# Output projection of a gated recurrent layer in half-precision parts, with a cast on ScalarE and a subtraction on GpSimd

## The chip, the core and the metric

The kernel runs on one core of a Trainium2 chip. Its time is the device time of one launch in microseconds (us), the median over several runs. The engines are TensorE (PE, and PEld for its weight loads), VectorE (DVE), ScalarE (ACT), GpSimd (POOL) and SyncE (SP). Each works through its own instruction stream in order, and the streams meet only at semaphores: an instruction may wait until a semaphore has reached a number, and may raise one when it is done.

## The reference, cut to what matters

The input x has 32 sequences of 128 positions with 256 features. A recurrent attention stand-in runs over the positions, then a mixture-of-experts feed-forward part follows.

```python
def step(carry, xs):                       # once for each of 128 positions
    r, state = carry
    r = decay * r + kt * vt
    retained = (qt * r).reshape(B, D)
    inp = retained @ Wi.T + bi
    gate = sigmoid(inp @ Wg.T + bg)
    blended = gate * state + (1.0 - gate) * inp
    state = tanh(blended @ A.T + inp @ Bm.T)
    out = state @ Wo.T + bo                # the projection that is changed
    return (r, state), out

x = x + tanh(g_xattn) * recurrence(layernorm(x), ctx, ctx)
x = x + tanh(g_ffn) * ffn(layernorm(x))
# ffn: silu(a) * b of a shared layer, times w_shared_out, plus the two best
# of eight experts on silu(a) * b of w1
```

## The kernel before, in words

**Tiles and iterations.** A tile is 8 positions of all 32 sequences: 256 tokens. There are 16. Data lie features on partitions, as two chunks of 128 features by 256 tokens, 128x512 in all. Iteration i works on several tiles at once: the eight recurrent steps of tile i; the input, gate and Bm products of tile a = i + 1, which don't depend on the state; the Wo projection, the second layer norm and the first shared product of tile c = i - 1; the rest of the feed-forward part of tile d = i - 2; and the first layer norm of tile f = i + 2. The last three tiles compute all experts (`DENSE`), the others scatter their rows to DRAM by expert, multiply block by block (`duo`, L621) and gather the results.

**The order.** The order on each engine is written out by hand in that engine's function `iteration`. Between two recurrent steps TensorE has filler work. After step 0 come the first half of w1 (L850) and perhaps a duo, after step 1 the Wo product (L862 to L869) and w1's second half (L872), which waits for `hs_ready`, after step 7 the second half of sh and the gate logits (L965 to L980).

**A recurrent step.** ScalarE makes the new state with a tanh (`tanh_step`, L999). VectorE makes from it u_hi (half precision), u_full and u_lo (`gated_state`, L1312). TensorE adds eight products with u_hi and four with u_lo to the addends in PSUM (`recurrence`, L593, lines 602 and 607).

**Half-precision parts.** Most products take their operands as hi + lo, two half-precision parts each, and sum hi x hi, hi x lo and lo x hi: `token_product` (L582, for tokens on the output's partitions) and `feature_product` (L567). The parts of an activation are made by a cast on ScalarE (hi) and a subtraction (lo), which is done on GpSimd by its helper `low` (L1856, the subtraction is line 1857) or on VectorE. The Wo product is an exception: float32 state times `whole_wo`, the float32 weights turned and scaled by ScalarE in the setup (L1169).

**Around the change.** ScalarE, behind the eighth tanh, takes the silu of the shared product into `sil_s` (L1274), in iterations 2 and 3 also a scale and a cast of w2 (`w2_high`, L1108). At the next iteration's start it presets the bank of the Wo product with the bias (`wo_preset`, L1031). VectorE, behind `gated_state(i, 7)`, does the routing sums (`rows`, in four iterations), the scan of the decaying memory (`scanned`, L1440, line 1445) and, in some iterations, additions of gathered rows (`combine_second`); in the next iteration it makes `hs` (L1671) behind `gated_state(i, 1)` and x1 from the Wo product (`projected`, L1482) behind `gated_state(i, 2)`. GpSimd starts the scatters (L1914) and gathers (L1927) at set steps (`moves`, L1952), each behind that step's tanh, and between them makes hs_lo (L1970), the low parts of hid (L1982, L1984) and, in iterations 2 to 4, those of w2 (`w2_low`, L1868).

## Time and profile before

| | |
|---|---|
| median of 3 runs | 471.37 us (470.33 to 474.23) |
| profiled execution | 472.12 us, its span 470.4 us |
| TensorE busy | 419.8 us, 89% |
| VectorE busy | 363.8 us, 77% |
| ScalarE busy | 226.1 us, 48% |
| GpSimd busy | 192.4 us, 41% |
| granted TensorE clock, mean | 0.985 of full speed |
| DMA | 63.08 MB, mean 134 GB/s |

A busy share is an average over the whole span. It says how much an engine does, not whether the end waits for it. What a shorter or a longer instruction is worth is read from the timeline around it: what the next instruction of each engine waited for. In a timeline row the first number is the start in us from the span's start, the second the duration in us; a bracket at the end gives the engine's idle time before the row and what ended it. Matmuls overlap each other, so their starts tell the pace and not their durations.

### The profile page before, as it was taken

The numbers are of one execution on the slowest core, as the hardware profiler recorded it, in microseconds if no ns is written. First come the engines' busy times: TensorE is split into PE (matmuls) and PEld (weight loads), VectorE is DVE, ScalarE is ACT, GpSimd is POOL, SyncE is SP. The second block draws the span as 40 slices with busy tenths as digits, with TensorE's granted clock in tenths as the row PEclk, the third lists the DMA queues.
The fourth block names the chain that finished last, engine by engine and source line by source line (L and its number), as shares of the span: only waits on it lengthen the run. The fifth ranks groups of instructions, "written<-read, shape, count | busy, mean of one in ns | idle before, by whom it ended". The sixth has DMA issues, their size and how long they took to land.

```text
span 470.4 us, 12307 instructions
## 1 busy us (share of the span) xinstructions
PE 419.8 (89%) x4348; PEld 353.8 (75%) x4348; DVE 363.8 (77%) x1305; ACT 226.1 (48%) x526; POOL 192.4 (41%) x231
## 2 busy tenths in 40 slices
PE   5987699999989999999999989997997998989891
PEld 4875487787878888889788878896986875766650
DVE  2687989999998887667988877769786569558784
ACT  3564556676655463546455546354653233321400
POOL 3011312432437530202275664431577463707551
PEclk9999899999999999999999999999999899999997
DMA  7795023325051655843423179793234859698862
GB/s 171 198 247 158 2 47 113 93 65 147 24 152 64 180 102 106 151 118 102 102 70 101 47 164 175 192 181 114 102 113 107 186 154 196 167 220 227 199 207 100
DMA packets 110283, 63.08 MB, mean 134 GB/s; under 512 B 80400, under 2 KB 100240, under 8 KB 110224
## 3 DMA queue, kind: packets, MB, share of 16 engines
q1 hardware_dynamic: 105104, 48.66, 43.6%
q0 software_dynamic: 5120, 13.64, 10.2%
q8 instruction: 36, 0.59, 0.5%
q14 instruction: 23, 0.19, 0.1%
HBM read 24.26 MB, written 27.53 MB: 110 GB/s over the span
## 4 chain that ended last, share of the span: by engine, by line
PE 46%; DVE 26%; issue 7%; DMA 6%; ACT 3%; POOL 3%; POOLq 0%; DVEq 0%; ACTq 0%
PE bank L577 9%; PE bank L588 9%; PE bank L635 9%; PE rec L719 4%; DVE u_hi L1324 4%; PE rec L602 4%; DVE u_full L1326 3%; DMA raw_sh<-hrows 2%; DVE r L1445 2%; PE rec L577 2%; PE bank L867 2%; PE rec L607 2%; DMA raw_w<-hrows 2%; PE bank L680 2%; DVE hs L1671 1%
## 5 line engine op out<-in xcount | busy, mean ns | idle before, releaser
L1004 ACT ACTIVATE state<-rec 128x64 f32<-128x64 f32 x128 | 36.7, 287 | 116.9 <-PE rec L607 115.7
L1914 POOL DMA_INDIRECT hrows<-hid_rows,slots_i x52 | 56.8, 1093 | 70.1 <-ACT state L1004 30.1
L1324 DVE SCALAR_TENSOR_TENSOR u_hi<-gt,state 128x64 f16<-128x64 f32 x127 | 43.0, 339 | 44.0 <-ACT state L1004 43.5
L1927 POOL DMA_INDIRECT yg<-yrows,slots_i x52 | 53.5, 1029 | 49.9 <-DMA yrows<-squares_sh 18.6
L602 PE MATMUL rec<-u_hi,a_hi 128*128 128x32 f16 x512 | 47.8, 195 | 14.7 <-DVE u_hi L1324 14.7
L602 PEld LDWEIGHTS rec<-u_hi,a_hi 128*128 128x128 f16 x512 | 37.0, 98 | 21.5 <-DVE u_hi L1324 19.0
L602 PE MATMUL rec<-u_hi,a_lo 128*128 128x32 f16 x512 | 47.5, 194 | 0.0
L1857 POOL TENSOR_TENSOR hs_lo<-hs,hs_hi 128x512 f16<-128x512 f32 x14 | 16.2, 1158 | 54.0 <-ACT hs_hi L1214 53.9
L607 PE MATMUL rec<-u_lo,a_hi 128*128 128x32 f16 x512 | 36.5, 194 | 1.6 <-DVE u_lo L1329 0.7
L1326 DVE SCALAR_TENSOR_TENSOR u_full<-gt,state 128x64 f32<-128x64 f32 x127 | 36.9, 290 | 0.0
L602 PEld LDWEIGHTS rec<-u_hi,a_lo 128*128 128x128 f16 x512 | 35.2, 98 | 1.6 <-issue 0.6
L577 PE MATMUL bank<-xn_hi,sh_hi 128*128 128x256 f16 x128 | 34.9, 273 | 0.0
L577 PE MATMUL bank<-xn_lo,sh_hi 128*128 128x256 f16 x128 | 34.9, 273 | 0.0
L577 PE MATMUL bank<-xn_hi,sh_lo 128*128 128x256 f16 x128 | 34.9, 273 | 0.0
L867 PE MATMUL bank<-whole_wo,state 128*128 128x256 f32 x128 | 32.9, 402 | 0.0
L1864 POOL TENSOR_TENSOR rs<-ve,minus_half 128x2 f32<-128x2 f32 x16 | 12.3, 770 | 49.5 <-DVE nm L1513 49.5
L635 PE MATMUL bank<-w_hi,raw_w 128*128 x144 | 27.2, 276 | 5.5 <-issue 3.3
L1329 DVE TENSOR_TENSOR u_lo<-u_full,u_hi 128x64 f16<-128x64 f32 x127 | 28.7, 226 | 4.3
L588 PE MATMUL bank<-w_hi,xn_hi 128*128 128x256 f16 x104 | 28.5, 274 | 3.0 <-DVE hs L1671 2.9
L719 PE MATMUL rec<-cn,whole_a 128*128 128x256 f32 x128 | 31.2, 387 | 0.0
L588 PE MATMUL bank<-w_lo,xn_hi 128*128 128x256 f16 x104 | 28.4, 273 | 0.0
L588 PE MATMUL bank<-w_hi,xn_lo 128*128 128x256 f16 x104 | 28.4, 273 | 0.0
(299 smaller groups left out, 1383.2 us busy)
## 6 DMA issues: line engine op xcount, KB each, us to landing
yrows<-squares_w SPq DMA_DIRECT2D x20, 256.0 KB, 3.0
yrows<-squares_sh SPq DMA_DIRECT2D x18, 256.0 KB, 3.1
x_sb<-in_x_dram SPq DMA_DIRECT2D x16, 256.0 KB, 3.4
c_sb<-in_ctx_dram SPq DMA_DIRECT2D x64, 64.0 KB, 3.1
xr_sb<-in_x_dram SPq DMA_DIRECT2D x16, 256.0 KB
hrows<-zeros SPq DMA_DIRECT2D x4, 1024.0 KB, 5.9
raw_w<-in_L_ffn_w_dram SPq DMA_DIRECT2D x8, 256.0 KB, 4.8
out_dram<-raw_w SPq DMA_DIRECT2D x8, 256.0 KB, 2.5
```

The lines of the kernel that those rows point to most:

```text
L577: last = pe.matmul(o, w[:, kc, at], a[:, kc, :], start=first, stop=(kc == KC - 1 and w is w_lo), skip_group_check=True)
L588: last = pe.matmul(dst, a[:, kc, s * P:(s + 1) * P], w(part, kc), start=first, stop=(kc == KC - 1 and a is a_lo), skip_group_check=True)
L602: pe.matmul(o[:, oc, :], w[:, kc, oc * P:(oc + 1) * P], u_hi[t % 2][:, kc, :], start=False, stop=False, skip_group_check=True)
L607: last = pe.matmul(o[:, oc, :], a16[0][:, kc, oc * P:(oc + 1) * P], u_lo[t % 2][:, kc, :], start=False, stop=(kc == KC - 1), skip_group_ch ...
L635: last = pe.matmul(dst[:, b * D:(b + 1) * D], hid_t[n % RING][:, half * KC + kc, b * P:(b + 1) * P], split["w2"][part][:, kc, bass.ds(e, 1 ...
L719: last = pe.matmul(rec[a % 2][:, oc, :], whole_a[:, kc, oc * P:(oc + 1) * P], cn[a % 2][:, kc, :], start=False, stop=(kc == KC - 1), skip_ ...
L867: last = pe.matmul(bank[B_WO][:, s * D:(s + 1) * D], state[c % 2][:, kc, s * P:(s + 1) * P], whole_wo[:, kc, :], start=False, stop=(kc == ...
L1004: act.activation(step_of(state[i % 2], t), step_of(rec[i % 2], t), ACT.Tanh, scale=1.0 / PSCALE).then_inc(st_ready, 1)
L1324: dve.scalar_tensor_tensor(out=u_hi[p][:, :, :], in0=gate, scalar=1.0, in1=old, op0=ALU.add, op1=ALU.mult).then_inc(uh_ready, 1)
L1326: dve.scalar_tensor_tensor(out=u_full[p][:, :, :], in0=gate, scalar=1.0, in1=old, op0=ALU.add, op1=ALU.mult).then_inc(uf_ready, 1)
L1914: pool.indirect_dma_start(hrows[q % 2], bass.IndirectOffsetOnAxis(ap=slots_i[q][:, at:at + 1], axis=0), hid_rows[t % 6][:, s, :, :].rearra ...
L1927: pool.indirect_dma_start(yg[t % FETCHED][:, s, pick, :], None, yrows[q % 2][0:blocks_of(q) * P, :], bass.IndirectOffsetOnAxis(ap=slots_i[ ...
```

## The change

The Wo product takes `wo` and the state in two half-precision parts each, through `token_product`: per half of the tokens 6 products of 256 columns in place of 2 float32 ones. The state's high part is a cast on ScalarE behind the eighth tanh (`state_high`), its low part a subtraction on GpSimd at the start of the next iteration (`state_low`). The first tanh of a tile waits for the low part of the tile two before and not for its Wo product. Wo's high part is made where `whole_wo` was, its low part by a new VectorE instruction in the setup, and the preset of the first bank waits for that. `hs` is written over `sil_s`, and the next silu of sh waits for hs_lo.

```diff
-        whole_wo = sb("whole_wo", [P, KC, D])
+        split["wo"] = (sb("wo_hi", [P, KC, D], F16), sb("wo_lo", [P, KC, D], F16))
...
+        st_s = (sb("st_hi", [P, KC, TOK], F16), sb("st_lo", [P, KC, TOK], F16))
...
-        hs = sb("hs", [P, KC, TOK])
+        hs = sil_s
...
                     pe.wait_ge(wo_bias, k.n(c))
-                    pe.wait_ge(st_ready, k.steps(c, STEPS))
+                    pe.wait_ge(st_hi, k.n(c))
+                    pe.wait_ge(st_lo, k.n(c))
                     for s in range(HALVES):
-                        for kc in range(KC):
-                            last = pe.matmul(bank[B_WO][:, s * D:(s + 1) * D], state[c % 2][:, kc, s * P:(s + 1) * P],
-                                             whole_wo[:, kc, :], start=False, stop=(kc == KC - 1), skip_group_check=True)
+                        last = token_product(bank[B_WO][:, s * D:(s + 1) * D],
+                                             lambda part, kc: split["wo"][part][:, kc, :], st_s, s, False)
                     last.then_inc(wo_done, 1)
...
                     if t == 0 and k.has(i - 2):
-                        act.wait_ge(wo_done, k.n(i - 2))
+                        act.wait_ge(st_lo, k.n(i - 2))
...
+            def state_high(i, k):
+                if not k.has(i):
+                    return
+                act.wait_ge(st_ready, k.steps(i, STEPS))
+                if k.has(i - 1):
+                    act.wait_ge(wo_done, k.n(i - 1))
+                act.copy(flat(st_s[0][:, :, :]), flat(state[i % 2][:, :, :])).then_inc(st_hi, 1)
...
                 if c == 0:
-                    act.wait_ge(setup_dve, 10)
-                    act.wait_ge(setup_act, 10)
+                    act.wait_ge(setup_dve, 11)
...
-            act.mul(flat(whole_wo[:, :, :]), bank[4][:, :], fold[:, 0:1]).then_inc(setup_act, 1)
+            act.mul(flat(split["wo"][0][:, :, :]), bank[4][:, :], fold[:, 0:1]).then_inc(setup_act, 1)
             tanh_step(0, 7, first)
+            state_high(0, first)
...
                 tanh_step(i, 7, k)
+                state_high(i, k)
                 if k.has(c):
                     act.wait_ge(sha_done, k.n(c))
                     if k.has(c - 1):
-                        act.wait_ge(hs_ready, k.n(c - 1))
+                        act.wait_ge(hs_lo, k.n(c - 1))
...
             gated_state(0, 7, first)
+            dve.wait_ge(setup_act, 10)
+            dve.scalar_tensor_tensor(out=flat(split["wo"][1][:, :, :]), in0=bank[4][:, :], scalar=fold[:, 0:1],
+                                     in1=flat(split["wo"][0][:, :, :]),
+                                     op0=ALU.mult, op1=ALU.subtract).then_inc(setup_dve, 1)
...
+            def state_low(c, k):
+                if not k.has(c):
+                    return
+                pool.wait_ge(st_hi, k.n(c))
+                if k.has(c - 1):
+                    pool.wait_ge(wo_done, k.n(c - 1))
+                low(flat(st_s[1][:, :, :]), flat(state[c % 2][:, :, :]), flat(st_s[0][:, :, :]), st_lo)
+
+            state_low(0, first)
...
                 c, d, f = i - 1, i - 2, i + 2
+                if c > 0:
+                    state_low(c, k)
                 moves(i, 0)
                 moves(i, 1)
```

## Rows read from the trace of the kernel before

**Rows 1.** The page, part 1: busy us, share of the span, instructions.

```profile
PE 419.8 (89%) x4348; PEld 353.8 (75%) x4348; DVE 363.8 (77%) x1305; ACT 226.1 (48%) x526; POOL 192.4 (41%) x231
```

**Rows 2.** Timeline of TensorE around tile 5's Wo product: start, duration, instruction.

```profile
158.67 0.28 PE L607 MATMUL rec<-u_lo,a_hi 128*128 128x32 f16 x4
158.78 1.97 PE L867 MATMUL bank<-whole_wo,state 128*128 128x256 f32 x8
160.93 0.28 PE L588 MATMUL bank<-w_hi,xn_hi 128*128 128x256 f16 x1 [0.17 <-DVE hs L1671]
161.04 0.27 PE L588 MATMUL bank<-w_lo,xn_hi 128*128 128x256 f16 x1
```

**Rows 3.** Timeline of VectorE in the same stretch.

```profile
156.49 1.35 DVE L1445 TENSOR_TENSOR_SCAN r<-dmask,c 128x576 f32<-128x576 f32 x1
...
159.44 0.27 DVE L1324 SCALAR_TENSOR_TENSOR u_hi<-gt,state 128x64 f16<-128x64 f32 x1
...
160.12 0.75 DVE L1671 SCALAR_TENSOR_TENSOR hs<-bank,hid_in,sil_s 128x512 f32<-128x512 f32 x1
```

**Rows 4.** Timeline of ScalarE in the same stretch.

```profile
155.47 0.29 ACT L1004 ACTIVATE state<-rec 128x64 f32<-128x64 f32 x1 [0.23 <-PE rec L607]
155.59 0.68 ACT L1274 ACTIVATE sil_s<-bank,in_un 128x512 f32<-128x512 f32 x1
...
160.96 0.62 ACT L1214 CAST hs_hi<-hs 128x512 f16<-128x512 f32 x1 [0.60 <-DVE hs L1671]
```

**Rows 5.** The waits: who waited for whom, us in total, times, longest.

```profile
PEld bank L588 <- DVE hs L1671: 8.2, 13, 1.1
```

**Rows 6.** Timeline of GpSimd around tile 5's Wo product.

```profile
156.54 2.08 POOL L1914 DMA_INDIRECT hrows<-hid_rows,slots_i  x1 [2.30 <-ACT state L1004]
158.92 0.97 POOL L1914 DMA_INDIRECT hrows<-hid_rows,slots_i  x1 [0.30 <-issue]
...
161.66 1.15 POOL L1857 TENSOR_TENSOR hs_lo<-hs,hs_hi 128x512 f16<-128x512 f32 x1 [0.49 <-ACT hs_hi L1214]
```

**Rows 7.** Timeline of all engines, tile 2, from its eighth tanh on.

```profile
90.42 0.28 ACT L1004 ACTIVATE state<-rec 128x64 f32<-128x64 f32 x1 [0.48 <-PE rec L607]
...
91.86 0.62 ACT L1114 CAST w_hi<-raw_w 128x512 f16<-128x512 f32 x1
...
92.56 1.19 POOL L1857 TENSOR_TENSOR w_lo<-raw_w,w_hi 128x512 f16<-128x512 f32 x1 [3.38 <-ACT w_hi L1114]
...
92.71 1.16 DVE L1324 SCALAR_TENSOR_TENSOR u_hi<-gt,state 128x64 f16<-128x64 f32 x1
...
96.79 0.28 PE L588 MATMUL bank<-w_hi,xn_hi 128*128 128x256 f16 x1 [0.32 <-DVE hs L1671]
```

**Rows 8.** Timeline of TensorE and VectorE: tiles 1, 6 and 12.

```profile
72.06 0.20 PE L602 MATMUL rec<-u_hi,a_hi 128*128 128x32 f16 x1 [0.28 <-DVE u_hi L1324]
...
178.10 0.27 DVE L1324 SCALAR_TENSOR_TENSOR u_hi<-gt,state 128x64 f16<-128x64 f32 x1
...
180.10 0.28 PE L607 MATMUL rec<-u_lo,a_hi 128*128 128x32 f16 x4
...
326.52 0.20 PE L602 MATMUL rec<-u_hi,a_hi 128*128 128x32 f16 x1 [1.29 <-DVE u_hi L1324]
```

**Rows 9.** Busy us (instructions) of PE, PEld, DVE, ACT, POOL, then clock, DMA share, GB/s.

```profile
50.15:53.30 3.15, 3.15 (x12) 2.32 (x11) 3.12 (x10) 2.16 (x4) 0.22 (x1) 0.57 0.00 0
...
360.00:364.00 4.00, 1.10 (x10) 0.75 (x10) 1.97 (x9) 0.68 (x2) 3.23 (x4) 1.00 0.95 197
364.00:368.00 4.00, 4.00 (x37) 3.44 (x37) 0.97 (x3) 1.27 (x3) 0.30 (x1) 0.57 1.12 151
```

**Rows 10.** Timeline of TensorE at tile 15's Wo product.

```profile
404.53 0.81 PE L867 MATMUL bank<-whole_wo,state 128*128 128x256 f32 x3
...
406.26 0.27 PE L577 MATMUL bank<-xn_hi,w_hi 128*128 128x256 f16 x1
```

**Rows 11.** Timeline of VectorE behind tile 0's eighth tanh.

```profile
48.32 0.22 DVE L1329 TENSOR_TENSOR u_lo<-u_full,u_hi 128x64 f16<-128x64 f32 x1
```

More of the change, by code:

```diff
@@ L298, in gated_layer @@
         wo_bias = sem("wo_bias")
+        st_hi, st_lo = sem("st_hi_ready"), sem("st_lo_ready")
         wo_done, x1_ready, ln2_stats, ln2_aggr, ln2_var, ln2_rstd, ln2_shift, xn2_ready = (
```

## The prediction, written before the changed kernel was run

> **What bounds the kernel now.** I read the page first: TensorE is busy 89% of the span and VectorE 77% [rows 1]. Such shares suggest that a shorter product shortens the kernel. So I went to the stretch where the changed product stands, in TensorE's timeline for tile 5, and asked what starts the work behind it [rows 2]. From here on "tile c" is the tile whose state is projected, and T is the end of its eighth tanh. For tile 5 T = 155.47 + 0.29 = 155.76 [rows 4].
>
> In rows 2 the last u_lo products of step 1 start at 158.67, the Wo product at 158.78, and the next work, the second half of w1, not before 160.93, with 0.17 us idle that VectorE's hs ended. VectorE's timeline says why [rows 3]. It takes the second tanh of the iteration, makes u_hi at 159.44, u_full and u_lo, and only then hs, 160.12 + 0.75 = 160.87. w1's second half starts 0.06 us after that. The Wo product stands inside a gap of 160.93 - 158.78 = 2.15 us that VectorE sets. The list of waits shows that this is the rule: the weight loads of L588 waited 13 times for hs [rows 5], and going through the timeline I find the next product starting 0.05 to 0.06 us behind hs in all fourteen tiles 1 to 14.
>
> **The product itself.** Now it is 4 float32 products in 8 records. In tile 15 it starts at 404.53 and the work behind it at 406.26, which is 1.73 us [rows 10]. The new one is 12 half-precision products of 256 columns. Such products follow each other by 161.04 - 160.93 = 0.11 us [rows 2], so 12 x 0.11 = 1.3 us, 0.4 to 0.5 us less. In tiles 1 to 14 hs is late by more than that, so TensorE only waits longer: saving 0. In tile 15 no recurrence and no hs stand behind it: 0.4 us saved. In tile 0 the stretch 50.15 to 53.30 has a granted clock of 0.57, most of it at 1.2 GHz, the lower level, and the product fills all 3.15 us [rows 9]. At the same clock the new one takes 1.31 / 0.57 = 2.3 us: 0.85 saved.
>
> **ScalarE's cast.** It is 128x512 float32 to half, like hs_hi, 0.62 us [rows 4]. It waits for its own tanh's completion, so it runs from about T + 0.03 to T + 0.65. Behind it in ScalarE's order stand the silu of sh, which started at T - 0.17 with 0.68 us and now ends at about T + 1.2, and the next tanh [rows 4]. The first half of w1 waits for that silu. TensorE gets there at about T + 1.36, so the cover holds by 0.1 us: cost 0. If it fails, 0.1 us a tile. In tiles 2 and 3 the w2 scale and cast stand there too, the cast ending at 91.86 + 0.62 = 92.48 and the tanh right behind it [rows 7]. There the shift of 0.7 us reaches the tanh.
>
> **GpSimd's low part.** Priced like hs_lo, 1.15 us, with a start 0.08 us after the ScalarE cast's end (160.96 + 0.62 to 161.66) [rows 4, 6]. So it starts at T + 0.73. Nothing waits for it soon, since the Wo product starts at about T + 3.0. The harm is on VectorE. In tile 2 a GpSimd subtraction of the same size runs from 92.56 to 93.75, and VectorE's u_hi, begun at 92.71, takes 1.16 us where 0.27 is usual [rows 3, 7]. It ends 0.12 us behind the subtraction. So this form of subtraction shuts out this form of VectorE work until it is over. The reverse is in rows 6: a scatter that starts at 156.54, 0.05 us behind the start of VectorE's 1.35 us scan, takes 2.08 us, the next one 0.97. The new low part starts at T + 0.73, and the scan at 156.49 = T + 0.73, a dead heat. Whichever is first, the other waits.
>
> The Trainium skill (SBUF — State Buffer, Who interferes with whom) states this as a rule: the pair of ports that VectorE and GpSimd share is an exclusive lock, and a VectorE instruction with two SBUF inputs contends with a GpSimd instruction that reads SBUF. The u_hi row agrees. By that rule tile 1 below costs its 0.9 us, without it nothing. The page also infers that writing DMA descriptors is not held up by such an input. The 2.08 us scatter goes against that.
>
> What a stall costs, by tile:
> - **Tiles 2, 3.** The profile has the price of one stalled u_hi: in tile 2 w1's second half starts at 96.79, with T = 90.70, at T + 6.09, in tile 5 at 160.93, T + 5.17 [rows 2, 7]. So 0.9 us is in there already. Now the w2 subtraction starts 0.7 us later and the low part queues right behind it (it is later in GpSimd's order). u_hi ends about T + 3.85, u_full or u_lo then waits for the low part, over at about T + 4.9, so the last u_lo products start near T + 5.2, not T + 3.7: 1.5 us each. Bounds 0.7 (the ScalarE shift alone) and 1.9 (shift and a full 1.15). Sum 3.0.
> - **Tile 1.** No duo, nothing else on GpSimd; TensorE already waits for u_hi at 72.06 [rows 8]. Low part and scan exclude each other: 0.9 (0 to 1.15).
> - **Tiles 4, 8, 12.** VectorE is late here by the routing sums or the additions of gathered rows. TensorE waits for u_hi, 1.29 us in tile 12 [rows 8] and in the same place in the other two. What VectorE loses is lost: 1.1 each, sum 3.3 (0.5 to 1.15 each).
> - **Tiles 6, 7, 14.** A duo stands between steps 0 and 1. In tile 6 u_hi starts at 178.10 and the u_lo products come at 180.10 [rows 8]: a delay of 1 us is hidden. 0.
> - **Tile 11.** Same cover, but VectorE adds gathered rows first and is later: 0.5, midway between 0 and 0.95.
> - **Tiles 5, 9, 10, 13.** GpSimd's order puts the last scatter of the iteration first. It ends at 156.54 + 2.08 = T + 2.86 [rows 6], the low part at about T + 4.0. The Wo product starts near T + 4.1 and ends at T + 5.4, the next start was T + 5.17: 0.25 each, sum 1.0. The low part is clear of the scan, and shuts u_hi at 159.44 out for some 0.3 us, which lies inside that.
> - **Tile 0.** VectorE is 0.4 us later behind T here, so that the low part at T + 0.73 comes just ahead of the u_lo at 48.32 [rows 11] and holds it up for 1 us; there is no filler work, and the new VectorE instruction for Wo's low part (0.75 us, as hs) stands before the next u_hi: 1.15 lost, less the 0.85 saved: 0.3.
> - **Tile 15.** -0.4.
>
> The rest costs nothing. hs over its silu is the same instruction on other addresses, and the next silu waits for hs_lo, over at 161.66 + 1.15 = 162.8, while that silu stands just ahead of the u_hi at 178.10 [rows 6, 8]. The first tanh of a tile waits for a low part made in the iteration before. Scatters and gathers queued behind the low part start up to 1.2 us later; GpSimd is busy 41% [rows 1] and their readers come iterations later.
>
> **Sum.** 0.3 + 0.9 + 3.0 + 3.3 + 1.0 + 0.5 - 0.4 = 8.6 us. The profiled execution took 472.12 us around a span of 470.4, which gives 480.7. It lies 0.75 above the median of the runs, 471.37, so against the median 480.0 us.
>
> **Rivals.**
> - **Mild (475.2 us).** Scan and low part run side by side, and the delays are partly absorbed: tile 1 0, tiles 2 and 3 0.7, tiles 4, 8 and 12 0.5, tile 11 0: 0.3 + 1.4 + 1.5 + 1.0 - 0.4 = 3.8. For it: no row shows a 128x512 subtraction beginning beside the scan, and the dead heat could fall well. Against it: the 2.08 us and the 1.16 us rows. 0.14.
> - **The saving reaches the end (463 us).** If the gap behind the Wo product were TensorE's own work and not hs, and the low part met no VectorE instruction, 16 x 0.5 = 8 us would go. The place is w1's second half in each tile; it decides from the point where that start follows the Wo product and not hs. Rows 2, 3 and 5 speak against it. 0.05.
> - **Harsh (486 us).** The upper bounds (tiles 2 and 3 0.8 more in all, tile 0 0.85, tile 11 0.45, the others 0.5 in all) and two further stretches like the one in rows 9: 3.4 us at half clock cost 1.7 each. For it: before the second such stretch, 364 to 368, TensorE was busy 1.10 of 4 us [rows 9], and it will idle more than now. Against it: the new waits are shorter than that. 8.6 + 2.6 + 3.4 = 14.6. 0.09.
> - The forecast itself: 0.72.
>
> About 1%, 4.7 us, is what a measurement of this kernel can tell from no change. Slower by more than that: the forecast and the harsh case and a little of the mild one, 0.82. Within: most of the mild case, 0.14. Faster: 0.04. The range goes from just under the mild case, 474.5, to 485.5.
>
> **What would show it.** The Wo product should be 12 records over 1.3 us, and the wait for hs behind it some 0.5 us longer in tiles 1 to 14. The low part should start at T + 0.7 in quiet tiles and at T + 2.9 in tiles 5, 9, 10 and 13, and overlap a u_hi, u_full, u_lo or scan of 1 us more than usual. The scan-to-u_hi stretch of tile 1 should be longer by 1 us, the stretch from T to w1's second half unchanged in tiles 6 and 7 and longest in 2 and 3. I am wrong if u_hi of the next step keeps its 0.27 us beside the low part, if T to w1's second half shrinks anywhere from 1 to 14, or if the delay is made good later in the iteration.

## The result: 490.0 us, slower by 3.6%

The changed kernel takes 490.04 us (488.64 to 492.11, 4 runs) beside 472.47 for the kernel before: a ratio of 1.0365 with a 95% interval of [1.0325, 1.0405]. Its profiled execution took 489.26 us around a span of 487.5. The forecast was 480.0, its range ended at 485.5. Of the 10 us between them 1.1 are the kernel before, whose median was 471.37 when the forecast was made. The direction was right, and so was the mechanism (GpSimd's subtraction holds up VectorE), but not where it acts. The loss in the traces was twice as large: 17.1 us of span where the sum had 8.6. All times and ratios leave out four executions in a slower state: one each of the kernel before and the memset kernel (497.3 and 479.2 us), two of the filled one (497.9 and 1464 us).

The page, part 1, of the changed kernel (columns as in [rows 1]):

```profile
PE 422.0 (87%) x4412; PEld 355.4 (73%) x4412; DVE 379.6 (78%) x1306; ACT 237.1 (49%) x542; POOL 215.3 (44%) x247
```

One VectorE instruction more makes VectorE 15.8 us busier than in [rows 1]. That is time in which its instructions were held up: with a memset in the subtraction's place (below) VectorE is back at 363.5 us. TensorE around tile 5's Wo product (compare [rows 2]):

```profile
168.61 0.29 PE L609 MATMUL rec<-u_lo,a_hi 128*128 128x32 f16 x4 [1.13 <-DVE u_lo L1341]
168.74 0.27 PE L590 MATMUL bank<-wo_hi,st_hi 128*128 128x256 f16 x1
...
169.94 0.27 PE L590 MATMUL bank<-wo_hi,st_lo 128*128 128x256 f16 x1
171.03 0.28 PE L590 MATMUL bank<-w_hi,xn_hi 128*128 128x256 f16 x1 [0.82 <-DVE sil_s L1687]
```

The product is 12 records over 169.94 + 0.11 - 168.74 = 1.3 us, as forecast. The gap behind it has grown from 0.17 to 0.82 us, ended by hs (now written over `sil_s`, L1687). The product saves nothing. What is new is TensorE's wait of 1.13 us for u_lo, just ahead of it. VectorE in that stretch (compare [rows 3]):

```profile
165.14 1.35 DVE L1457 TENSOR_TENSOR_SCAN r<-dmask,c 128x576 f32<-128x576 f32 x1
...
166.89 1.67 DVE L1341 TENSOR_TENSOR u_lo<-u_full,u_hi 128x64 f16<-128x64 f32 x1
...
170.22 0.75 DVE L1687 SCALAR_TENSOR_TENSOR sil_s<-bank,hid_in,sil_s 128x512 f32<-128x512 f32 x1
```

And GpSimd (compare [rows 6]):

```profile
165.19 2.08 POOL L1940 DMA_INDIRECT hrows<-hid_rows,slots_i  x1 [2.31 <-ACT state L1006]
167.28 1.18 POOL L1873 TENSOR_TENSOR st_lo<-state,st_hi 128x512 f16<-128x512 f32 x1
```

u_lo takes 1.67 us where [rows 11] show 0.22. It began 0.39 us before the low part's recorded start and ended 0.1 us behind it, at 168.56. The forecast had the low part at T + 2.9, and it stands there (T = 164.40). What it meets is the u_lo ahead of it, which the forecast had as done by then.

Tile 1, all engines, where scan and low part meet:

```profile
71.80 2.31 POOL L1873 TENSOR_TENSOR st_lo<-state,st_hi 128x512 f16<-128x512 f32 x1 [9.86 <-ACT st_hi L1040]
71.81 1.35 DVE L1457 TENSOR_TENSOR_SCAN r<-dmask,c 128x576 f32<-128x576 f32 x1
73.08 1.58 DVE L1850 SCALAR_TENSOR_TENSOR so_lo<-raw_so,fold,so_hi 128x512 f16<-128x512 f32 x1
```

The dead heat goes to the scan, which keeps its 1.35 us. The low part waits inside its 2.31 us and then shuts out what VectorE has behind the scan. In tile 1 that is so_lo, which takes 1.58 us instead of the 0.72 of the kernel before; in tiles 6 and 7 it is u_hi, 1.16 and 1.17. The forecast had the exclusion for tile 1, at 0.9 us; it cost 0.85.

Tile 2 (compare [rows 7]), GpSimd and TensorE:

```profile
96.12 1.15 POOL L1873 TENSOR_TENSOR w_lo<-raw_w,w_hi 128x512 f16<-128x512 f32 x1 [4.11 <-ACT w_hi L1124]
97.23 1.19 POOL L1873 TENSOR_TENSOR st_lo<-state,st_hi 128x512 f16<-128x512 f32 x1
...
98.86 0.29 PE L609 MATMUL rec<-u_lo,a_hi 128*128 128x32 f16 x4 [1.00 <-DVE u_lo L1341]
```

The u_lo products start at T + 5.3 (T = 93.54), forecast T + 5.2. Tile 13, TensorE:

```profile
366.90 0.27 PE L590 MATMUL bank<-wo_hi,st_hi 128*128 128x256 f16 x1 [2.30 <-POOL st_lo L1873]
```

Here GpSimd has three scatters between T and the low part, and not one. The Wo product waits for it and starts at T + 5.5 (T = 361.41); forecast was T + 4.1. The waits of the changed kernel, us in total, times, longest (compare [rows 5]):

```profile
PEld bank L590 <- DVE sil_s L1687: 11.7, 12, 1.4
PEld rec L609 <- DVE u_lo L1341: 11.6, 26, 1.2
PE bank L590 <- DVE sil_s L1687: 7.9, 10, 1.2
PE rec L609 <- DVE u_lo L1341: 7.9, 9, 1.1
```

In the kernel before, the weight loads waited 8.2 us for hs and 4.3 for u_lo. The last thing is the clock. The trace of the kernel before has two half-clock stretches (1.2 instead of 2.4 GHz) ahead of its end, each 3.4 us long ([rows 9]). The trace of the changed one has seven, 34.1 us together. Three of them (columns as in [rows 9]):

```profile
99.45:102.87 3.42, 3.42 (x18) 2.17 (x16) 3.18 (x13) 1.85 (x4) 0.87 (x1) 0.50 0.00 0
123.35:126.77 3.42, 3.39 (x17) 2.11 (x16) 3.12 (x12) 1.82 (x3) 0.93 (x1) 0.50 0.02 5
379.35:386.17 6.82, 5.98 (x42) 5.04 (x43) 1.63 (x7) 1.30 (x3) 1.54 (x3) 0.50 0.96 182
```

These two traces overstate the difference. The mean granted clock was 0.985 in the trace of the kernel before, but 0.975 on average over 66 other executions of it; it was 0.956 in this trace of the changed kernel and 0.963 on average over ten. A microsecond at half clock takes half a microsecond off the mean, so the remaining 0.012 of 490 us is, as an estimate, some 12 us more at half clock, and not the 27 that the two traces show.

**Where the time went.** For each tile the time from its T to the next tile's, changed minus before, in two traces of the changed kernel (the second is from the last experiment):

| tiles projected | forecast | first trace | second trace |
|---|---|---|---|
| 0 | 0.3 | 2.3 | 1.2 |
| 1 | 0.9 | 0.85 | 0.86 |
| 2, 3 | 3.0 | 4.9 | 3.3 |
| 4, 8, 12 | 3.3 | 2.9 | 2.9 |
| 5, 9, 10 | 0.75 | 3.7 | 4.0 |
| 6, 7, 14 | 0 | 0.2 | 0.25 |
| 11 | 0.5 | 0.7 | 0.7 |
| 13 | 0.25 | 2.8 | 3.2 |
| 15 to the end, and before tile 0 | -0.4 | -1.1 | 1.5 |
| sum | 8.6 | 17.1 | 17.9 |

Tile 10 counts less to the next T than to w1's second half, where all of 5, 9 and 10 stand 1.45 us later than before. Before its fourth tanh TensorE waits there for rows that a DMA brings, 1.2 us in the kernel before and 0.5 here, and that takes up some of the delay.

### The profile page after: what moved, and what is told of

It reads as the page before. It is cut to its first block, busy times and chain, and to the rows that moved or that the text cites. A ratio compares the mean times of both kernels' runs of the same rounds, so it can differ in the third digit from the quotient of the medians.

```text
span 487.5 us, 12497 instructions
## 1 busy us (share of the span) xinstructions
PE 422.0 (87%) x4412; PEld 355.4 (73%) x4412; DVE 379.6 (78%) x1306; ACT 237.1 (49%) x542; POOL 215.3 (44%) x247
## 4 chain that ended last, share of the span: by engine, by line
PE 43%; DVE 29%; issue 9%; POOL 5%; ACT 4%; DMA 3%; POOLq 0%; DVEq 0%; ACTq 0%
PE bank L590 10%; PE bank L579 8%; PE bank L637 8%; PE rec L721 4%; DVE u_hi L1336 4%; DVE u_full L1338 3%; PE rec L604 3%; DVE r L1457 2%; PE rec L579 2%; PE rec L609 2%; DVE u_lo L1341 2%; DVE sil_s L1687 2%; POOL hrows L1940 2%; ACT state L1006 2%; DVE ret L1470 1%
## 5 line engine op out<-in xcount | busy, mean ns | idle before, releaser
L1336 DVE SCALAR_TENSOR_TENSOR u_hi<-gt,state 128x64 f16<-128x64 f32 x127 | 45.4, 358 | 45.7 <-ACT state L1006 45.3
L1873 POOL TENSOR_TENSOR st_lo<-state,st_hi 128x512 f16<-128x512 f32 x16 | 22.5, 1409 | 49.7 <-ACT st_hi L1040 49.6
L1338 DVE SCALAR_TENSOR_TENSOR u_full<-gt,state 128x64 f32<-128x64 f32 x127 | 39.7, 312 | 0.0
L1341 DVE TENSOR_TENSOR u_lo<-u_full,u_hi 128x64 f16<-128x64 f32 x127 | 35.7, 281 | 4.4
L590 PE MATMUL bank<-w_hi,xn_hi 128*128 128x256 f16 x104 | 29.5, 283 | 8.1 <-DVE sil_s L1687 7.9
L637 PE MATMUL bank<-w_hi,raw_w 128*128 x144 | 29.3, 289 | 4.8 <-issue 3.9
L721 PE MATMUL rec<-cn,whole_a 128*128 128x256 f32 x128 | 33.2, 406 | 0.0
L609 PEld LDWEIGHTS rec<-u_lo,a_hi 128*128 128x128 f16 x512 | 23.7, 99 | 12.2 <-DVE u_lo L1341 11.6
```

The source lines that it names most:

```text
L590: last = pe.matmul(dst, a[:, kc, s * P:(s + 1) * P], w(part, kc), start=first, stop=(kc == KC - 1 and a is a_lo), skip_group_check=True)
L609: last = pe.matmul(o[:, oc, :], a16[0][:, kc, oc * P:(oc + 1) * P], u_lo[t % 2][:, kc, :], start=False, stop=(kc == KC - 1), skip_group_ch ...
L637: last = pe.matmul(dst[:, b * D:(b + 1) * D], hid_t[n % RING][:, half * KC + kc, b * P:(b + 1) * P], split["w2"][part][:, kc, bass.ds(e, 1 ...
L721: last = pe.matmul(rec[a % 2][:, oc, :], whole_a[:, kc, oc * P:(oc + 1) * P], cn[a % 2][:, kc, :], start=False, stop=(kc == KC - 1), skip_ ...
L1336: dve.scalar_tensor_tensor(out=u_hi[p][:, :, :], in0=gate, scalar=1.0, in1=old, op0=ALU.add, op1=ALU.mult).then_inc(uh_ready, 1)
L1338: dve.scalar_tensor_tensor(out=u_full[p][:, :, :], in0=gate, scalar=1.0, in1=old, op0=ALU.add, op1=ALU.mult).then_inc(uf_ready, 1)
```

## The experiments

**The parts without the product.** The changed kernel makes st_hi and st_lo, but multiplies float32 with `whole_wo` as before; Wo's low part is not made.

```diff
-                    pe.wait_ge(st_hi, k.n(c))
-                    pe.wait_ge(st_lo, k.n(c))
+                    pe.wait_ge(st_ready, k.steps(c, STEPS))
...
-                        last = token_product(bank[B_WO][:, s * D:(s + 1) * D],
-                                             lambda part, kc: split["wo"][part][:, kc, :], st_s, s, False)
+                            last = pe.matmul(bank[B_WO][:, s * D:(s + 1) * D], state[c % 2][:, kc, s * P:(s + 1) * P],
+                                             whole_wo[:, kc, :], start=False, stop=(kc == KC - 1), skip_group_check=True)
```

> The changed kernel with the Wo product of before: float32 state times whole_wo, no low part of Wo. The cast and the subtraction of the state are still made, and no product reads them. If VectorE's time behind GpSimd's subtraction is the loss (my theory), this is as slow as the changed kernel: 484 to 490 us, u_lo of tiles 5, 9 and 10 still near 1.7 us, only the 1.6 us wait for the low part in tile 13 gone. If the twelve half-precision products are the loss (rival), it falls back to 471 to 475 us. If the wait for a late low part were most of it (second rival), about 475 us too.

Measured: 487.13 us, ratio 1.0278 [1.025, 1.0306], as forecast. Most of the loss is there with no product waiting for the low part: 2.8% beside the 3.7% and, measured again below, 3.3% of the changed kernel. Tiles 1, 4, 5, 8, 9 and 12 lose 0.87, 0.97, 1.44, 0.97, 1.45 and 0.90 us, within 0.04 of the changed kernel. In these tiles the loss is what making the parts does to VectorE. Even tile 13, whose Wo product waits for nothing here, has w1's second half at T + 6.69 (T = 360.17), beside T + 6.80 in the changed kernel and T + 5.18 before. Its VectorE, GpSimd and TensorE:

```profile
363.87 1.79 DVE L1338 SCALAR_TENSOR_TENSOR u_hi<-gt,state 128x64 f16<-128x64 f32 x1
```

```profile
363.35 0.98 POOL L1938 DMA_INDIRECT hrows<-hid_rows,slots_i  x1 [0.30 <-issue]
364.33 1.19 POOL L1871 TENSOR_TENSOR st_lo<-state,st_hi 128x512 f16<-128x512 f32 x1
```

```profile
366.86 0.28 PE L590 MATMUL bank<-w_hi,xn_hi 128*128 128x256 f16 x1 [1.69 <-DVE sil_s L1685]
```

u_hi is held for 1.79 us, from 0.46 us before the low part's recorded start, and hs with it. So the 2.30 us wait of the changed kernel's Wo product lies beside the same stall of VectorE and adds 0.1 us to it. That doesn't make the wait harmless: it would bound the tile without the stall too, as the third experiment shows.

**The product without the low part.** `state_low` is not called and the high part stands in for the low one, so the kernel leaves out the low part of the state and its output is another.

```diff
-                    pe.wait_ge(st_lo, k.n(c))
...
-                                             lambda part, kc: split["wo"][part][:, kc, :], st_s, s, False)
+                                             lambda part, kc: split["wo"][part][:, kc, :], (st_s[0], st_s[0]), s, False)
...
-                if c > 0:
-                    state_low(c, k)
```

> The changed kernel without the state's low part: GpSimd makes none, the product takes the high part in its place (12 products of the same size), so the output lacks that part. My theory: the product saves nothing against before and ScalarE's cast costs nothing, so the time is that of the kernel before within 0.5%, 469 to 473 us, the start of w1's second half stays at T + 5.2 in tiles 5, 9, 10 and 13, the wait for hs in front of it grows to 0.7 us, and the granted clock is back above 0.98. Rival, ScalarE's cast in the way of the silu and the tanh: 474 to 480 us, worst in tiles 2 and 3. Rival, the faster product does pay once the subtraction is gone: 463 to 466 us.

Measured: 472.77 us, ratio 0.999 [0.9963, 1.0018], as forecast. Tile 5 again (T = 156.37):

```profile
159.40 0.27 PE L590 MATMUL bank<-wo_hi,st_hi 128*128 128x256 f16 x1
...
160.60 0.27 PE L590 MATMUL bank<-wo_hi,st_hi 128*128 128x256 f16 x1
161.54 0.28 PE L590 MATMUL bank<-w_hi,xn_hi 128*128 128x256 f16 x1 [0.67 <-DVE sil_s L1686]
```

w1's second half starts at T + 5.17, as before to the hundredth, behind 0.67 us idle instead of 0.17: saving 0. Tiles 2 and 3 lose 0.70 and 0.69 us, the shift of ScalarE that the forecast had as their lower bound. All other tiles up to 12 stay within 0.1 us. Tile 13 loses 0.74 and tile 14 gains 0.35, and the stretch before tile 0 is 0.83 us shorter.

**A one-column memset ahead of the low part**, in tiles 5, 9, 10, 11, 13, 14 and 15, with a wait for its completion, so that the low part is not queued right behind the scatter.

```diff
+                if c in (5, 9, 10, 11, 13, 14, 15):
+                    fences.append(c)
+                    pool.memset(fence[:, :], 0.0).then_inc(fenced, 1)
+                    pool.wait_ge(fenced, len(fences))
```

> The changed kernel with a one-column memset on GpSimd, and a wait for its end, ahead of the low part of tiles 5, 9, 10, 11, 13, 14 and 15, where a scatter or gather stands right before it. Theory: a subtraction queued behind a scatter shuts VectorE out while the scatter still runs. Then the u_lo of tiles 5, 9 and 10, now 1.67 us, is back at 0.23, the loss of each of them falls from 1.45 to about 0.3 us, and the time is 484 to 487 us. Rival: the scatter's own tail is what holds u_lo; then u_lo stays above 1 us and the time at 489 to 491 us.

Measured: 490.6 us, 1.0366 [1.0332, 1.04], where 484 to 487 was forecast. VectorE and GpSimd at tile 5:

```profile
164.35 0.23 DVE L1341 TENSOR_TENSOR u_lo<-u_full,u_hi 128x64 f16<-128x64 f32 x1
...
165.57 0.67 DVE L1336 SCALAR_TENSOR_TENSOR u_hi<-gt,state 128x64 f16<-128x64 f32 x1
```

```profile
162.67 2.08 POOL L1947 DMA_INDIRECT hrows<-hid_rows,slots_i  x1 [2.31 <-ACT st_hi L1040]
164.74 0.13 POOL L1922 MEMSET fence<- 128x1 f32 x1
164.95 1.15 POOL L1873 TENSOR_TENSOR st_lo<-state,st_hi 128x512 f16<-128x512 f32 x1
```

u_lo is back at 0.23 us, and tiles 5 and 9 lose 0.79 and 0.77 us instead of 1.46 and 1.45. Most of what they still lose is at u_hi, which meets the low part and takes 0.67. So being queued right behind the scatter is what takes the u_lo. It is not that VectorE is always held some 0.4 us ahead: in tile 13 of this trace a u_lo that began 0.19 us before the low part took its 0.22.

The total did not follow: tile 13 lost 4.6 us and the end 3.2. Tile 13, TensorE, T = 356.77, and VectorE at hs:

```profile
362.42 0.27 PE L590 MATMUL bank<-wo_hi,st_hi 128*128 128x256 f16 x1 [2.46 <-POOL st_lo L1873]
```

```profile
361.13 0.75 DVE L1687 SCALAR_TENSOR_TENSOR sil_s<-bank,hid_in,sil_s 128x512 f32<-128x512 f32 x1
```

VectorE is not held up here, its u_hi takes 0.27 us and hs is over at T + 5.1. But the low part still comes late, so the Wo product starts at T + 5.65, and its 1.3 us alone would put w1's second half at T + 7.0. So in tile 13 the late low part is a second cause beside the stall, and taking away either leaves the other. That the tile lost 4.6 us, and not 2.8 as in the first trace of the changed kernel, goes with the clock: a half-clock stretch begins at 362.76, 0.34 us behind the wait, and puts w1's second half at T + 7.88.

**The low part a queue place earlier**, ahead of its tile's last scatter (twice: the second time in one call with the changed kernel).

```diff
-                if c > 0:
-                    state_low(c, k)
...
                 for t in range(5, STEPS):
+                    if t == STEPS - 1:
+                        state_low(i, k)
                     moves(i, t)
```

> The changed kernel with the low part queued on GpSimd ahead of its tile's last scatter instead of behind it. Theory (the stall of VectorE in tiles 5, 9, 10 comes from a two-input subtraction that is queued right behind a running scatter, and in tile 13 the projection waits for the low part behind two scatters): the wait of 2.3 us for the low part in tile 13 is gone, u_lo in tiles 5, 9, 10 is back near its 0.23 us, and tiles 5, 9, 10 lose 0.9 us each instead of 1.45, tile 13 0.9 instead of 1.6; together some 2 us, so 487 (485 to 489). The scatter itself goes 1.2 us later, which costs nothing unless the gather behind it is waited for. Rival (the low part stalls VectorE by its full length wherever it lies, and the low clock is what remains): 489 to 490, no difference from the changed kernel's 490.

> The same kernel as e9_low_before_scatter. Its profiled execution lay 2.0 us below the changed kernel's, as its tiles 5, 9, 10 and 13 say, but the medians of four runs only 0.3. If what the tiles show reaches the end: 487.5 to 488.5, some 2 us below e14_changed_again on the same chip. If the low clock takes it back: 489.5 to 490.

Measured: 489.75 us (1.0364 [1.0325, 1.0402]) and 488.77 (1.032 [1.0281, 1.036]), the changed kernel beside the second 489.27. Tile 5, VectorE and GpSimd:

```profile
163.35 1.16 DVE L1336 SCALAR_TENSOR_TENSOR u_hi<-gt,state 128x64 f16<-128x64 f32 x1
...
164.72 0.22 DVE L1341 TENSOR_TENSOR u_lo<-u_full,u_hi 128x64 f16<-128x64 f32 x1
```

```profile
162.08 2.30 POOL L1873 TENSOR_TENSOR st_lo<-state,st_hi 128x512 f16<-128x512 f32 x1 [2.25 <-ACT st_hi L1040]
164.54 1.02 POOL L1940 DMA_INDIRECT hrows<-hid_rows,slots_i  x1 [0.16 <-issue]
```

Now tile 5 has tile 1's pattern, and loses 0.91 and 0.90 us in the two traces, tile 9 as much: what the theory said of the tiles. Tile 13's Wo product no longer waits for the low part, and the third tanh of its iteration is late by 0.9 us more than T in both traces, instead of 1.6 and 3.2 in those of the changed kernel. But tile 10 shows 1.57 and 1.32, and tile 13 to the end of its iteration 2.56 and 2.95, with a half-clock stretch of 6.8 us in it. In tile 10 w1's second half stands at T + 6.1, as in 5 and 9, and the rest comes at the wait for the rows, here 1.83 and 1.56 us long, 1.2 in the kernel before:

```profile
288.62 0.28 PE L637 MATMUL bank<-w_hi,raw_w 128*128 x1 [1.83 <-DMA raw_w<-hrows]
```

The scatters stand behind the low part now and go later. That this is why the rows come later isn't shown, since the wait also varies where they don't (at most 0.3 us in the memset's trace). Over the ten runs of each, the changed kernel has a mean of 489.6 us and this one 489.2, with a standard deviation of 1.7: the difference of 0.4 is not resolved. The gain in tiles 5 and 9 is shown; 2 us at the end, which both expectations had, are not.

**A memset in place of the subtraction**: same place and waits, written but nothing read (the low part is zero).

```diff
-                low(flat(st_s[1][:, :, :]), flat(state[c % 2][:, :, :]), flat(st_s[0][:, :, :]), st_lo)
+                pool.memset(flat(st_s[1][:, :, :]), 0.0).then_inc(st_lo, 1)
```

> The changed kernel with a memset of the low part's tile on GpSimd in the place of the subtraction: same tile, same waits, but nothing is read from SBUF (the output lacks the state's low part). If reading through the port that VectorE's second input needs is what shuts VectorE out (my theory), the scan and u_full of tile 4 and the u_lo of tile 0 keep their usual 1.35, 0.27 and 0.23 us beside it, and the time is 472 to 475 us, as without the low part. Rival: any GpSimd instruction on a tile of this size does it, or the added waits do; then u_full and u_lo beside it grow by the memset's length and the time is 478 us or more.

Measured: 473.88 us, 1.0008 [0.9973, 1.0042], as forecast. Tile 5, GpSimd and VectorE:

```profile
157.45 2.08 POOL L1940 DMA_INDIRECT hrows<-hid_rows,slots_i  x1 [2.30 <-ACT state L1006]
159.52 0.55 POOL L1920 MEMSET st_lo<- 128x512 f16 x1
```

```profile
159.13 0.23 DVE L1341 TENSOR_TENSOR u_lo<-u_full,u_hi 128x64 f16<-128x64 f32 x1
```

In tile 4 the memset runs beside u_full (two inputs in SBUF), GpSimd and VectorE:

```profile
135.16 0.53 POOL L1920 MEMSET st_lo<- 128x512 f16 x1 [2.20 <-ACT st_hi L1040]
```

```profile
135.31 0.27 DVE L1338 SCALAR_TENSOR_TENSOR u_full<-gt,state 128x64 f32<-128x64 f32 x1
```

Right behind the same scatter nothing is held up, and u_full keeps 0.27 us, where the changed kernel's takes 1.23 beside the subtraction. Tiles 1, 4, 5, 8 and 9 lose at most 0.05 us; tile 10, with a shorter wait for its rows, gains 1.1, and tile 13 loses 1.1. It is GpSimd's reading of SBUF that costs, not its being busy. That is the rule of the Trainium skill (SBUF — State Buffer, Who interferes with whom), by which a VectorE instruction with two SBUF inputs does not contend with a GpSimd instruction that only writes SBUF; this trace agrees.

**The low part in the window where VectorE reads one SBUF input**, behind the u_lo of the next iteration's step 1.

```diff
+                if k.has(c + 1):
+                    pool.wait_ge(ul_ready, k.steps(c + 1, 1) + 1)
```

> The changed kernel with the low part of tile c held back until VectorE has made the u_lo of step 1 of the next tile, so that it runs at about T + 2.8 to T + 4.0, beside VectorE instructions with one SBUF input. Theory: u_hi, u_full, u_lo and the scan of steps 0 and 1 then keep their usual lengths, only the step-1 u_hi is held some 0.3 us, and the Wo product waits 1 us in the gap that hs sets anyway: 0.3 us lost per tile, 1.7 in all of tiles 2 and 3 to the ScalarE shift, 476 to 480 us. Rival: the late low part costs as much as the collisions did, 486 us or more.

Measured: 489.05 us, 1.0361 [1.027, 1.0451]: 9 us above the forecast's upper end. The stalls of VectorE at the low part are gone but for a u_hi of 0.42 to 0.51 us in most tiles (and 1.80 in tile 13, where nothing had moved), and in their place TensorE waits (tile 5):

```profile
166.35 0.27 PE L590 MATMUL bank<-wo_hi,st_hi 128*128 128x256 f16 x1 [1.01 <-POOL st_lo L1873]
```

Tile 1 loses 0.17, but tiles 4, 8 and 12 1.6 to 1.9 us, and the trace has nine half-clock stretches ahead of its end (mean clock 0.949).

**The low part on VectorE**, behind the first gated state of the iteration; GpSimd makes none.

```diff
                 gated_state(i, 0, k)
+                if k.has(c):
+                    dve.wait_ge(st_hi, k.n(c))
+                    if k.has(c - 1):
+                        dve.wait_ge(wo_done, k.n(c - 1))
+                    low(flat(st_s[1][:, :, :]), flat(state[c % 2][:, :, :]), flat(st_s[0][:, :, :]), st_lo)
```

> The changed kernel with the state's low part made by VectorE, behind its work for step 0 of the next tile, in place of GpSimd. A 128x512 subtraction of two SBUF inputs takes VectorE 0.67 us. If VectorE sets the pace between steps 0 and 2 (my theory), each of the tiles 1 to 14 loses 0.5 to 0.7 us, less in 6, 7, 11 and 14, and tiles 2 and 3 another 0.7: 479 to 483 us, still 6 us or more under the changed kernel. Rival: VectorE has that much room, 473 to 476 us.

Measured: 479.42 us, 1.0139 [1.0077, 1.0201], as forecast. Tiles 5, 8, 9 and 10 lose 0.57 to 0.63 us each, tiles 1 and 12 0.92 and 1.24, which is no less than with GpSimd. In all the same subtraction costs less than half on the fuller engine, 1.4% beside 3.3 to 3.7%.

**hs ahead of the next gated state**, in the kernel before; then also `ld` behind `x_stats` (twice).

```diff
                 retained(a, k)
+                if k.has(d):
+                    ...
+                    dve.scalar_tensor_tensor(out=flat(hs[:, :, :]), in0=bank[B_SHB][:, :], scalar=hid_in[:, 0:1],
+                                             in1=flat(sil_s[:, :, :]), op0=ALU.mult, op1=ALU.mult).then_inc(hs_ready, 1)
```

The old place of hs, behind `gated_state(i, 1)`, is empty then. The second kernel has this besides:

```diff
                 ret_low(a, k)
+                x_stats(f, k)
                 if k.has(d):
...
                     dve.tensor_tensor(ld[:, :, :], top[:, :, :], top[:, :, 0:1].to_broadcast([P, HALVES, E]),
                                       ALU.subtract).then_inc(ld_ready, 1)
-                x_stats(f, k)
```

> The kernel before with hs made by VectorE ahead of the step 1 state work and not behind it; all else as before. If hs is what the work behind the Wo product waits for (my theory), w1's second half starts right behind the Wo product, at T + 4.9 in place of T + 5.2, 0.3 us saved in about ten tiles: 466 to 469 us. Rival: hs only delays u_hi of step 2, and recurrence 2 waits: 471 to 476 us.

> The kernel before with hs ahead of the step 1 state work, as in the run before, and ld behind the statistics of x, so that no two-input instruction stands on VectorE while GpSimd makes hs_lo. In the run with hs early alone ld took 1.13 us beside hs_lo and u_hi of step 2 was 0.4 us late. If that is what took the gain back (theory): 466 to 469 us. Rival: VectorE's sum of work between steps 1 and 4 is the limit, whatever the order: 470 to 473 us.

> The same kernel as e8_hs_early_ld_late (float32 projection; hs ahead of the next gated state, ld behind x_stats), in five rounds to narrow its ratio of 0.993. If the gain is real: 468 to 471 us, a ratio of 0.990 to 0.996 with an interval below 1. If it came of where the low clock fell in those runs: 472 to 473, a ratio of 1.

Measured: hs alone 472.47 us, 0.9983 [0.9962, 1.0005], no gain where 466 to 469 was forecast. With `ld` later 470.0, 0.993 [0.9893, 0.9967] (forecast 466 to 469), and again 469.88, 0.9936 [0.9905, 0.9966]: 0.7% faster than the kernel before, little but with both intervals below 1. hs is done inside the Wo product and the gap behind the product is gone (tile 5, TensorE, T = 155.47):

```profile
158.51 1.97 PE L867 MATMUL bank<-whole_wo,state 128*128 128x256 f32 x8
...
160.32 0.27 PE L588 MATMUL bank<-w_hi,xn_hi 128*128 128x256 f16 x1
```

With hs alone the low part of hs runs beside `ld` (1.13 us long there), and T to w1's second half is as short, but tile 5 as a whole gains nothing; with `ld` moved it gains 0.34 us. So the meeting of `ld` and the low part of hs had taken the gain.

**The same two moves, with the half-precision product and no low part; and with its low part on VectorE.** Both are made of the kernels above by the same edit. The first again leaves out the state's low part.

> No low part (Wo is multiplied with the high part twice, so the output is another), and hs of a half is made ahead of the next gated state, with ld behind x_stats as in e8_hs_early_ld_late. Question: is the half-precision product's shorter time worth anything once hs is no longer what ends behind it? Theory (TensorE then sets the pace, and the 12 half-precision matmuls are shorter than the float32 product by some 0.3 to 0.5 us a tile): 463 to 467 us, below e8_hs_early_ld_late's 470. Rival (VectorE's own work between two tanhs sets the pace, the product lies beside it): 469 to 471, as e8_hs_early_ld_late.

> The half-precision projection with its low part made by VectorE (as in e7_low_on_vector), and hs ahead of the next gated state with ld behind x_stats. Theory (the low part costs 0.6 us a tile on VectorE, and the early hs gives back 0.2 to 0.5 us a tile as it did in e8_hs_early_ld_late): 475 to 478 us. Rival (the early hs and the low part stand in each other's way at the same place of VectorE's queue, so that nothing is given back): 479 or more.

Measured: without a low part 466.04 us, 0.9864 [0.9827, 0.99]. Between the T of tiles 5 and 13 it gains 5.1 us on the kernel before, the float32 version with the same moves 2.2 and 2.3 in its two traces. The difference, 2.9 us in eight tiles, is 0.36 each: the 0.4 us that the forecast had between the two products. With the low part on VectorE 471.64 us, 0.997 [0.9947, 0.9993]: 3.4 us below the 475 to 478 expected, level with the kernel before, 1.8 above the float32 version. The product's saving is real once hs is early (466.04 beside 469.88 us), and the low part costs more than it (471.64 beside 466.04).

**TensorE's new waits filled** with matmuls that add zero, and the changed kernel beside it, once more.

```diff
+            def filler(n):
+                for m in range(n):
+                    pe.matmul(bank[B_WO][:, 0:D], zeros[:, 0:P], zeros[:, 0:D], start=False, stop=False, skip_group_check=True)
```

> The changed kernel with TensorE's new waits filled: half-precision matmuls with zero weights (0.11 us each, adding zero to the Wo bank) stand where the changed kernel's trace has TensorE idle in step 1 of the iteration: 7 to 14 ahead of the wait for u_hi in tiles 1 to 4 and 8, 8 or 9 ahead of the wait for u_lo in tiles 2, 3, 5, 9 and 10, 18 ahead of the wait for st_lo in tile 13. They end about when the wait did. Theory (the half-clock stretches of iterations 4, 5 and 14, at 99.45, 123.35, 338.39 and 379.35 us of the changed kernel, follow from these waits, and cost some 0.75 us each, the last 1.3): those stretches gone, 486.5 to 488. Rival (the clock falls for another reason, and filling costs a little where a matmul outlasts the wait): 490 to 491, stretches as before.

> The changed kernel itself once more, on the same chip as the two beside it and with a second trace: 489 to 491. Its trace shows which half-clock stretches come again (those that a wait of this kernel brings should stand in the same iterations, those that don't should move).

Measured: filled 491.66 us, 1.0375 [1.0324, 1.0426], where the theory had 486.5 to 488; the changed kernel 489.27, 1.0328 [1.0287, 1.0368]. The filler buys nothing. In the changed kernel's second trace the stretches near 99 and 123 us did not come, and tiles 2 and 3 lost 3.3 us instead of 4.9: each had cost 0.8. Since the waits are in both traces, and no stretch is there in the unfilled one, the filled kernel shows nothing about these two. A third stretch did come, from 366.1 on, right behind the 2.30 us wait of tile 13; with 18 fillers in that wait it did not. Second trace of the changed kernel, then the filled one, same stretch:

```profile
365.50:369.50 4.00, 4.00 (x33) 3.15 (x30) 1.32 (x5) 0.62 (x1) 2.98 (x3) 0.58 0.19 66
```

```profile
365.50:369.50 4.00, 4.00 (x53) 3.75 (x51) 2.45 (x9) 1.39 (x3) 3.38 (x4) 1.00 0.19 66
```

Instead the filled kernel has a 6.8 us stretch at 377, as the first trace of the changed one at 379: its tile 13 lost 4.3 us. That the wait of tile 13 brings the stretch isn't shown: one came behind it in the second trace and behind the 2.46 us wait of the third experiment, but none in the first trace, which has the same 2.30 us. The stretches of iteration 14 don't go away with the wait.

## Why the prediction was wrong

Right, with their numbers: the saving of 0 (within 0.1 us in tiles 1 and 4 to 12 of the second experiment); the exclusion of scan and low part; tile 1 (0.9, measured 0.85); tiles 4, 8, 12 (1.1 each, 0.9 to 1.0); tiles 6, 7, 14 (0, at most 0.15); tile 11 (0.5, 0.7); tiles 2 and 3 at full clock (1.5 each, 1.65). The rival in which the saving reaches the end fell with the second experiment, and the mild one with tile 1. The measured time lies above the harsh one too.

**The step that failed is the term for tiles 5, 9, 10 and 13**, "0.25 each, sum 1.0", and in it the clause that the low part "shuts u_hi at 159.44 out for some 0.3 us". I took the low part's effect to begin with its row. A two-input subtraction queued right behind a scatter holds VectorE from before its recorded start: u_lo 1.67 us. Tiles 5, 9 and 10 cost 3.7 to 4.0 us against 0.75, shown by the one-column memset (u_lo 0.23) and the earlier queue place (0.9 in tiles 5 and 9). Why the effect starts early isn't shown; recorded starts on GpSimd are rough, so part of the 0.39 us may be the record's.

**Tile 13** is in the same term, with a miscount of GpSimd's queue on top. Three scatters in a row stand behind T there (361.9 to 365.6 in the changed kernel), so the low part came at T + 4.2 and held u_hi, and hs behind it. T to w1's second half rose from 5.2 to 6.8 us. I first read this as TensorE's wait for the low part, the 2.30 us. The first experiment, where no product waits for it, shows 6.7 us by VectorE's stall alone; the third, where VectorE isn't held, would have 7.0 by the wait alone. Either is enough for the 1.6 of the 2.8 us. The other 1.2 come later in iteration 14, where the half-clock stretch is 6.8 us long and was 3.4.

**The clock** I had left to a rival, at two stretches more and 0.09, and the sum had nothing for it. The argument against the rival was that the new waits are shorter than the one in rows 9. It doesn't hold as a reason: stretches came behind waits of 2.30 and 2.46 us, though not each time. What stretches cost I can give by rows only where two traces differ: 1.6 us for the two in tiles 2 and 3 (1.3 for the two there in the two traces of the earlier queue place), 1.1 for the longer one in tile 0, and 1.8 in tile 13 between the two traces of the float32 kernel with hs and `ld` moved, -0.3 with a stretch of 3.4 us and +1.5 with 6.8. That long stretch of iteration 14 is in seven of the eight traces with the subtraction on GpSimd and in one of the nine others, so it goes with the change; how, isn't shown. The first trace's excess over the forecast is 17.1 - 8.6 = 8.5 us, tile by tile: 2.9 in tiles 5, 9 and 10, 2.5 in tile 13, 1.9 in tiles 2 and 3, 2.0 in tile 0, and -0.8 in the rest. What sets the spread of the end (tile 15 and after: from -0.8 to +3.2 in the traces of kernels that make the low part on GpSimd) stays open. The three with 2.5 us or more there, and no others of them, have a half-clock stretch near 434.5 us. How much of iteration 14's loss is clock alone stays open too.

## What to carry to other kernels

Before shortening an instruction, find what starts the work behind it; here VectorE's hs did, so 0.4 us a tile were worth nothing until hs was moved. Moving hs and `ld` in the kernel before, without the change, gained 3 us; hs alone gained nothing. A subtraction on the emptier engine is not free when it reads SBUF beside VectorE's two-input instructions: in tiles 5, 8 and 9 it cost 1.0 to 1.5 us on GpSimd (44% busy) and 0.6 on VectorE (78%). Count the queue of the engine that takes new work in every iteration, not in one, and price the instruction ahead of the new one on the other engine as well as the one behind.

## What the runs showed of the hardware

- A 128x512 subtraction on GpSimd right behind a scatter lengthened a VectorE subtraction that had begun 0.39 us before it (1.67 us instead of 0.23), and a gated state that had begun 0.46 us before (1.79 instead of 0.27). Behind a gather, in tile 14, a u_lo begun 0.69 us before took 1.94. With a one-column memset between, or with a memset in its place, it did not.
- A scan and a GpSimd subtraction that start together: the scan keeps 1.35 us, the subtraction shows 2.31 instead of 1.15. A scatter that starts 0.05 us behind the scan (tiles 5, 9, 10) shows 2.08 instead of 0.97; the gather that starts with the scan of tile 11 (294.52 in the kernel before) shows 1.00.
- A 128x512 half-precision memset on GpSimd takes 0.53 to 0.55 us and holds nothing up, beside the scan and u_full too.
- Half-clock stretches come and go between executions of one kernel (near 99 and 123 us: in one trace of two of the changed kernel, and in one of two of the earlier queue place), worth 0.7 to 0.8 us each.
